# A gated state-space layer on one core: the second convolution tile moved to the gate's PSUM bank, and taps, z split and output product moved in the chunk step

## The reference

```
proj = xn @ in_proj.T                       # gate (4096), x (4096), B, C (8 x 128 each), dt (64)
x, B, C = silu(causal_conv4(proj))          # 4 taps per channel
state_t = state_(t-1) * exp(dt_t A) + dt_t x_t B_t
y_t = state_t C_t + D x_t                   # 64 heads of 64, in 8 groups
z = y * rsqrt(mean(y^2 in its group) + eps) * norm_weight * silu(gate)
out = z @ out_proj.T ;  x = x + out
```

## Time and profile before

| | |
|---|---|
| median of 3 runs | 1332.53 us (1332.19 to 1333.8) |
| profiled execution, its own time | 1333.64 us |
| its span, first to last instruction | 1331.9 us |
| mean granted TensorE clock | 0.979 of full speed |
| TensorE / VectorE / ScalarE / GpSimd busy | 1239.0 / 926.7 / 691.6 / 658.7 us |
| groups 1 to 6, each | 117.9 us |
| groups 0 and 7 with the handover | 61.9 to 176.3 us, 883.9 to 1008.0 us |

### The profile page before, as it was taken

One profiled execution on the slowest core, in us unless ns is written; L12 is line 12 of the kernel. 1 busy time (PEld: TensorE's weight loads), 2 busy tenths in 40 slices (PEclk: granted clock), 3 DMA queues, 4 the chain that ended last, 5 costly groups with the idle time before them and its releaser, 6 DMA issues.

```text
span 1331.9 us, 22035 instructions
## 1 busy us (share of the span) xinstructions
PE 1239.0 (93%) x6680; PEld 966.3 (73%) x6690; DVE 926.7 (70%) x1734; ACT 691.6 (52%) x1042; POOL 658.7 (49%) x707
## 2 busy tenths in 40 slices
PE   5999999999999999999999999998878999889976
PEld 4777777776777777777777777776666777667764
DVE  5786677667667766766776676677766655569995
ACT  3675666566656656675666567555523333222220
POOL 5056546654744665475465456543663434343330
PEclk9999999999999999999999999999989999999996
DMA  5111011011101201110010110010003233131100
GB/s 174 45 49 34 1 51 48 18 33 48 32 1 32 64 16 32 48 30 3 32 64 16 32 48 25 9 37 1 22 27 107 83 95 98 44 94 35 56 16 24
DMA packets 44233, 57.52 MB, mean 43 GB/s; under 512 B 10117, under 2 KB 21159, under 8 KB 43929
## 3 DMA queue, kind: packets, MB, share of 16 engines
q1 hardware_dynamic: 44185, 56.92, 14.0%
HBM read 49.95 MB, written 6.96 MB: 43 GB/s over the span
## 4 chain that ended last, share of the span: by engine, by line
PE 68%; DVE 11%; issue 9%; ACT 7%; POOL 2%; DMA 1%; DVEq 1%; SPq 1%; ACTq 0%; POOLq 0%
PE p_d L94 14%; PE p_d L98 7%; PE p_gate L94 6%; PE p_tile L94 5%; PE p_in L1092 4%; PE p_x L1100 4%; DVE conv L702 3%; PE p_y L1121 3%; PE p_gate L98 3%; PE p_tile L98 2%; PE t_p_a L1872 2%; PE p_y L94 2%; ACT L612 2%; PE t_p_c L1940 2%; PE p_in L94 2%
## 5 line engine op out<-in xcount | busy, mean ns | idle before, releaser
L702 DVE SCALAR_TENSOR_TENSOR conv<-p_tile,conv_taps,conv 128x511 f32<-128x511 f32 x189 | 141.4, 748 | 46.2 <-ACT conv L573 31.2
L812 DVE TENSOR_TENSOR em<-em,p_gb 128x512 f32<-128x512 f32 x128 | 82.1, 682 | 65.7 <-ACT em L612 65.7
L702 DVE SCALAR_TENSOR_TENSOR conv<-p_d,conv_taps,conv 128x511 f32<-128x511 f32 (+2 forms) x99 | 73.9, 747 | 65.8 <-ACT conv L573 61.9
L94 PE MATMUL p_d<-wr_hi,zt_hi 128*128 128x512 f32 x248 | 101.1, 408 | 13.1 <-DVE wr_lo L740 7.9
L94 PE MATMUL p_tile<-xn_hi,wc_hi 128*128 128x512 f32 x252 | 110.1, 437 | 0.8 <-DVE halo L706 0.8
L578 ACT ACTIVATE xbc<-conv 128x512 f32<-128x512 f32 x96 | 60.6, 631 | 94.2 <-DVE conv L710 57.9
L516 POOL TENSOR_TENSOR squares<-squares 128x256 f32<-128x256 f32 x64 | 47.7, 746 | 122.2 <-ACT squares L635 122.2
L485 POOL TENSOR_TENSOR x_w<-xs,head_g 128x512 f32<-128x512 f32 x56 | 59.2, 1057 | 98.3 <-ACT xs L606 97.8
L94 PE MATMUL p_gate<-xn_hi,wr_hi 128*128 128x512 f32 x248 | 104.2, 420 | 0.0
L635 ACT ACTIVATE squares<-y 128x512 f32<-128x512 f32 x64 | 40.5, 633 | 119.8 <-DVE y L845 116.4
L94 PE MATMUL p_tile<-xn_lo,wc_hi 128*128 128x512 f32 x252 | 98.5, 391 | 0.0
(11 more groups left out here) (361 smaller groups left out, 3511.8 us busy)
## 6 DMA issues: line engine op xcount, KB each, us to landing
w_raw<-w SPq DMA_DIRECT2D x108, 256.0 KB, 2.7
q_words<-q SPq DMA_DIRECT2D x33, 256.0 KB, 2.6
h_ring<-h_lo_rows SPq DMA_DIRECT2D x6, 704.0 KB, 4.8
h_lo_rows<-h_rest SPq DMA_DIRECT2D x11, 256.0 KB, 2.0
x_res<-x SPq DMA_DIRECT2D x8, 256.0 KB, 4.8
out<-out_t SPq DMA_DIRECT2D x8, 256.0 KB, 2.0
h_lo_rows<-h_rest SPq DMA_DIRECT2D x11, 128.0 KB, 1.8
gate_second<-w SPq DMA_DIRECT2D x4, 256.0 KB, 5.2
```

The source lines that it names most:

```text
L94: pe.matmul(out, lhs(k)[0], rhs(k)[n], start=(start and k == 0 and n == 0), stop=False)
L702: ve.scalar_tensor_tensor(out=conv[:, s, sh:], in0=p[:, 0:HALF - sh], scalar=conv_w[:, bass.ds(g, 1), j, tap], in1=conv[:, s, sh:], op0=AL ...
L812: ve.tensor_tensor(m, m, gm.unsqueeze(1).broadcast_to([P, HG // 2, P]), ALU.mult)\
```

## The change

Five edits, in all engines' programs at once:

1. The second convolution tile of a step (j = 1, 3) goes to p_gate; the gate product of a two-tile step goes to p_tile. Their waits follow: the second tile waits for the gate's silu or the previous tile's taps, the gate product for the first tile's taps.
2. VectorE takes the last taps of the second tile at the start of the next step (in step 0 all but the first tap), and ScalarE's silu of it comes there too, behind the exponentials. The decay product no longer waits for them.
3. z is rounded and split in its own step, right after the z product, not in the next one.
4. In two-tile steps the output product stands behind the second tile; elsewhere it stands ahead of the state product, now in the last half group too. The residual comes after the z product (in the last half group before y is summed); the row sum comes later (or, in the last half group, earlier and in another bank).
5. Of the four output weight tiles ScalarE rounds 12, 13, 10, 11 in one go in step 0; GpSimd scales and splits 12 and 13 (`out_rest`), VectorE splits 10 and 11. `norm` and the addition of x_d change places on GpSimd.

```diff
-    def out_bank(last, c):
-
-        return p_y if last and c == NC - 1 else p_d0
+    def ss_bank(last, c):
+
+        return p_gate[:, 0:1] if last and CH <= c < NC else p_gb[:, 3 * P:3 * P + 1]
+
+    def gate_bank(c):
+
+        return p_tile if c % CH < 2 else p_gate
 
     def bank_of(j):
...
-        return (p_tile, p_d1)[j in (1, 3)]
+        return (p_tile, p_gate)[j in (1, 3)]
...
-    VE_LO = list(range(TILES + KT, WT))
-    POOL_LO = list(range(TILES + KT))
-    FIRST = [0, 1, 2, 3, 6, 7, 8, 9, 4, 5]
+    OUT = TILES + KT
+    VE_LO = [OUT, OUT + 1]
+    POOL_LO = list(range(OUT)) + ["scaled", OUT + 2, "scaled", OUT + 3]
+    FIRST = [0, 1, 2, 3, 6, 7, 8, 9, 4, 5] + POOL_LO[OUT:]
+    ROUNDED = [OUT + 2, OUT + 3, OUT, OUT + 1]
...
-        return g * WT + (FIRST.index(w) if is_zero(g) and w in FIRST else w) + 1
+        if w >= OUT:
+            return g * WT + OUT + ROUNDED.index(w) + 1
+        return g * WT + (FIRST.index(w) if is_zero(g) else w) + 1
...
+                if c == 0:
+                    for w in (OUT + 2, OUT + 3):
+                        out_rest(g, w)
+                if last and c >= CH:
                     norm(n - 1, (c - 1) % 2)
                 if c > 0:
 
                     pool.wait_ge(s_t, st)
                     pool.wait_ge(s_xd, n + 1)
                     pool.tensor_tensor(y[:], y[:], x_d[:], ALU.add).then_inc(s_txd, 1)
-                if tail:
+                if not (isinstance(g, int) and n == 0) and not (last and c >= CH):
...
+        def out_rest(g, w):
+
+            raw = w_raw[:, w % RAW, :]
+            scale = norm_w[:, bass.ds(g, 1), w - OUT].broadcast_to([P, D])
+            pool.wait_ge(s_whi, hi_count(g, w))
+            pool.tensor_tensor(raw, raw, scale, ALU.mult).then_inc(s_wlo, 1)
+            done, count = lo_count(g, w)
+            pool.wait_ge(done, count - 1)
+            pool.tensor_tensor(lo_of(w), raw, hi_of(w).bitcast(F32), ALU.subtract).then_inc(s_wlo, 1)
...
-        up.rest(pool, 0, 0, 0)
         rstd_of(NC - 2)
         sum_squares(LAST)
+        up.rest(pool, 0, 0, 0)
         norm(LAST, (NC - 1) % 2)
...
-                for tile in left:
-                    tile_silu(*tile)
                 act.wait_ge(s_xt, n + 1)
                 wait(act, s_xdt, n)
                 act.activation(xs[:], p_x[:], ACT.Copy).then_inc(s_xs, 1)
-                if not first:
-                    z_round(n - 1, p_y)
...
+                for tile in left + now:
                     tile_silu(*tile)
                 for T, tg, j, _ in later:
                     tile_in(T, tg, j)
                 if c == 0:
                     wait(act, s_out, n)
-                    w_round(g, TILES + KT)
-                    w_round(g, TILES + KT + 1)
+                    for w in ROUNDED:
+                        w_round(g, w)
                 act.wait_ge(s_y, n + 1)
                 wait(act, s_ss, n)
                 act.activation(squares[:], y[:], ACT.Square).then_inc(s_sq, 1)
+                z_round(n, y_bank(last, c))
                 made = gate_tile(g, last, c)
                 if made:
-                    wait(act, s_z, n)
-                    gate_silu(CH + n, made[1], made[2])
-                if c == 0:
-                    w_round(g, TILES + KT + 2)
-                    w_round(g, TILES + KT + 3)
+                    gate_silu(CH + n, made[1], made[2], gate_bank(c))
...
-        z_round(LAST, y_bank(True, NC - 1))
+        up.round_w(act, 0, 0, 0)
...
-                _, now, later = conv_tiles(g, last, c)
+                left, now, later = conv_tiles(g, last, c)
                 tail = last and c >= CH
 
                 ve.wait_ge(s_gb, n + 1)
                 wait(ve, s_m, 2 * n)
                 ve.tensor_tensor(gm, p_gb[:, 0:P], tri[:], ALU.mult).then_inc(s_gm, 1)
                 ve.tensor_copy(b_tok[:], p_gb[:, P:2 * P]).then_inc(s_gm, 1)
-                if not first:
-                    z_rest(n - 1, p_y)
+                for tile in left:
+                    tile_taps(*tile, range(1 if c == 1 else 2, TAPPED[tile[3]]))
+                if tail:
+                    variance(n - 1, (c - 1) % 2, ss_bank(last, c))
                 for k in rows_in(last, c):
...
-                if not first and not tail:
-                    variance(n - 1, (c - 1) % 2)
+                if tail:
+                    residual(n - 1, c - 1)
+                    row_stats(c - 1)
...
-                if tail:
-                    variance(n - 1, (c - 1) % 2)
-                elif not first:
-                    residual(n - 1, (c - 1) % NC, p_d0)
                 for tile in later:
                     tile_taps(*tile, range(1))
-                if last and c == NC - 1:
-                    up.scale(ve, 0, 0, 0)
+                if not first and not tail:
+                    variance(n - 1, (c - 1) % 2, ss_bank(last, c))
...
-                if tail:
-                    residual(n - 1, c - 1, out_bank(last, c))
+                if not first and not tail:
+                    residual(n - 1, (c - 1) % NC)
                 for k in rows_in(last, c):
                     row_rest(k)
+                if last and c == NC - 1:
+                    up.scale(ve, 0, 0, 0)
+                z_rest(n, p)
...
-                if last and c > 0:
+                if last and 0 < c < CH:
                     row_stats(c - 1)
...
-                for tile in later:
-                    tile_taps(*tile, range(1, TAPPED[tile[3]]))
                 if c == 0:
-                    for k in range(GW // P):
-                        w_rest(g, TILES + KT + k)
+                    for w in VE_LO:
+                        w_rest(g, w)
+                else:
+                    for tile in later:
+                        tile_taps(*tile, range(1, 2))
...
-        z_rest(LAST, y_bank(True, NC - 1))
-        variance(LAST, (NC - 1) % 2)
+        variance(LAST, (NC - 1) % 2, ss_bank(True, NC))
...
+        def conv_tile(T, g, j, hf, bank=None, made=0):
+
+
+            if bank is not None:
+                wait(pe, s_tap, TAPS * (j - 1))
+            elif j in (1, 2, 4):
+                wait(pe, s_sg, made)
             else:
-                wait(pe, s_tap, TAPS * (j - 1))
+                wait(pe, s_tap, tapped(g, hf, {3: 2}.get(j, j)))
...
+                tg, j, hf = tile
+                if c % CH < 2:
+                    pe.wait_ge(s_tap, tapped(tg, hf, 2 * j) + TAPPED[hf])
+                elif c % CH == 2:
+                    pe.wait_ge(s_tap, tapped(tg, hf, 4))
+                else:
+                    pe.wait_ge(s_sg, CH + n)
+                gate_product(*tile, gate_bank(c))
+
+        def sum_rows(m, ss):
...
-                for _, tg, j, hf in left:
-                    pe.wait_ge(s_tap, tapped(tg, hf, j) + TAPPED[hf])
...
-                    conv_tile(*tile)
-                if c == 1:
-                    pe.wait_ge(s_whi, (g + 1) * WT)
-                    pe.wait_ge(*lo_count(g, WT - 1))
-                if not first and not tail:
+                    conv_tile(*tile, made=CH + n)
+                if tail:
+                    pe.wait_ge(s_sg, LAST + 1)
+                    wait(pe, s_v, n - 1)
+                    sum_rows(n - 1, ss_bank(last, c))
+                if not first and not later:
                     pe.wait_ge(s_e, 2 * n + 1)
                     out_product(n - 1, p_d0)
-                    pe.wait_ge(s_m, 2 * (n + 1))
-                    sum_rows(n - 1)
...
-                if last and c == NC - 1:
-                    pe.wait_ge(s_e, 2 * (n + 1))
-                    pe.wait_ge(s_res, n - 1)
-                    up.spread(pe, 0, 0, 0)
-                if later:
-                    pe.wait_ge(s_e, 2 * (n + 1))
                 for tile in later:
-                    conv_tile(*tile)
+                    conv_tile(*tile, made=CH + n)
+                if c == 1:
+                    pe.wait_ge(s_whi, (g + 1) * WT)
+                    for w in (VE_LO[-1], WT - 1):
+                        pe.wait_ge(*lo_count(g, w))
+                if not first and later:
+                    pe.wait_ge(s_e, 2 * n + 1)
+                    out_product(n - 1, p_d0)
 
                 pe.wait_ge(s_m, 2 * (n + 1))
-                if tail:
-                    sum_rows(n - 1)
+                if not first and not tail:
+                    sum_rows(n - 1, ss_bank(last, c))
...
-                if tail:
-                    if c < NC - 1:
-                        pe.wait_ge(s_e, 2 * (n + 1))
-                    out_product(n - 1, out_bank(last, c))
                 next_gate(g, last, n, c)
...
-        pe.wait_ge(s_sg, LAST + 1)
+        pe.wait_ge(s_res, LAST)
+        up.spread(pe, 0, 0, 0)
+        pe.wait_ge(s_v, LAST)
         pe.wait_ge(l2_lo, NC - 2)
         up.spread(pe, 0, 1, 1)
+        sum_rows(LAST, ss_bank(True, NC))
+        out_product(LAST, p_y)
         row_transpose(NC - 2, LAST)
-        sum_rows(LAST)
-        out_product(LAST, p_y)
```

36 lines of the change are left out of this document (11 added, 25 removed).

## The result

The changed kernel takes 1338.31 us (median of 15 runs, 1334.06 to 1339.94); the kernel before took 1332.66 beside it (15 runs, 1331.80 to 1334.34). The ratio is 1.0036, with a 95% interval from 1.0028 to 1.0044: slower by 0.36%. The prediction was 1318, in a range from 1303 to 1329, with 0.10 for slower. It was wrong in sign and outside its range.

A forecast was written before the change was run, and what follows sets the result against it. TensorE, busy 93% of the span, was taken as the bound, with only idle and low-clock time to win. Groups 1 to 6 -4.6, group 0 -1.2, group 7 -0.1, last half group -9: -14.9, giving 1318, range 1303 to 1329.

The forecast's parts named there:

- The second tile's bank: Second tile in p_gate: decay product no longer waits for its taps, nothing lost; steps 2, 5, 6 gain 2.77 per group.
- The chain from step 0 to step 1: Late output product, ScalarE rounding, four GpSimd instructions, norm, then residual: step 1's decay product starts at 312.7, unhindered 309.9.
- The length of step 1: Middle groups' step 1 becomes 20.0 instead of 18.08, 2.0 lost; bounds 18.5 and 21.0.
- the lower bound: Step 1 of the middle groups if the chain meets no contention: 18.5, 0.5 lost.
- Group 0: Step 1 taken unchanged; -0.8 for step 2 and -0.4 for steps 5 and 6, together -1.2.
- Step 4: No cost taken; longer than 15.7 would mean a late gate silu or residual, margin only 0.3 to 0.6 us.
- The last half group: Output product fills TensorE's gap before the transposes: step 4 to 10.0, steps 4 to 6 to 33.0; -9 taken with handover.
- may fall as often as before: In the last half group the clock may fall as often as before, giving -5.0 instead of -12.0.
- -5 to -12 for the tail: Last half group with handover: -12.0 at full clock, -5.0 by the clock column; -9 taken.
- The weak tail: Rival: VectorE's queue and low clock limit the last half group to -4, 1323 in all, or 1329 without group gains; chance 0.2.
- the dear scaled product: Rival: GpSimd's one-value-per-partition product costs more than 1.06; at 3.0 us, step 1 grows 3.9, time 1345; chance 0.1.
- the listed signs: If right: residual wait 2 to 3, tap wait 1 to 2 in step 1, GpSimd full, steps 2 and 6 full.
- the signs that it is wrong: Step 1 under 18 or over 21 us; steps 0 and 4 longer than 14.6 and 15.7.

The follow-up runs named there:

- The first experiment: Changed kernel with GpSimd making the norm in step 0 ahead of its four output weight instructions; 1313.7 us, ratio 0.9855.
- the four built on it: On the norm-first kernel: decayed state early, 1316.2 us; that with old last half group, 1317.5; decayed state plus later VectorE rest, 1308.8; that plus two tail moves, 1304.1.
- the last one: Changed kernel with only two last-half-group moves: squares ahead of rstd on GpSimd, row splits ahead of y and z on VectorE; 1330.5 us, ratio 0.9978.
- The two moves of the last experiments: Last half group: GpSimd squares ahead of rstd and decayed state, VectorE row splits ahead of y and z; 1304.1 us with earlier edits, 1330.5 alone on changed kernel.
- the fastest one: Changed kernel with norm and decayed state early on GpSimd, one VectorE rest behind step 1's left taps, and two last-half-group moves; 1304.1 us, ratio 0.978.
- the kernel with the decayed state early: Norm-first kernel with GpSimd also making step 1's decayed state in step 0, ahead of norm and output weight rests; 1316.2 us, ratio 0.9881.

## Why the prediction was wrong

The forecast sum was -14.9 us, and the span grew by 5.6. Two terms of the sum carry most of the 20.5 us between them: the last half group with its handover (11.3) and groups 1 to 6 (6.9).

*The second tile's bank.* Right. The wait for taps before the decay product is gone and nothing took its place in steps 2, 3, 5 and 6. The six steps other than 1 and 4 give 3.2 per group where 2.77 was forecast.

*The chain from step 0 to step 1.* Its mechanism was right in each link, and its first length too: the decay product was forecast 2.8 late and waits 2.71. GpSimd's four instructions take 4.95 plus gaps where 5.0 with 0.45 for contention was put. The first experiment, which takes the norm out of this chain, shows it: the wait goes everywhere.

*The length of step 1.* This is the term that was mis-sized: 21.1 on average, not 20.0, so 3.0 lost per group, not 2.0 (20.0 - 18.08 is 1.92; the sum took 2.0). That is 6.1 us more than forecast in groups 1 to 6, where 6.9 was missed in all; step 4, below, adds 3.4, and the other six steps take off 2.5. Two sizes failed. The short taps were put at 1.05; they took 3.38 in three of the groups (2, 3 and 6), where GpSimd's weight rests of step 1 lie beside them, and the second tile waited 2.36, not 1.5. And the sum kept TensorE at full clock, since the earlier trace rows shows 1.00 in every step: in seven of the eight groups it fell once in step 1, at 1.5 us each. Groups 1, 4 and 5 took the forecast 20.0 by luck, for another reason than forecast: no wait for taps (18.5, the lower bound), plus one fall of the clock. In the middle groups the fall needs the 2.71 wait: in the kernel with the norm first, the four built on it, and the one with four splits on VectorE, which all remove it, the clock falls in no step 1 of groups 1 to 6. But the wait does not make the fall certain, since group 6 of the changed kernel has both long waits and no fall, and it is not the only thing that brings one: group 0 has no such wait, only waits of 0.21, 0.45 and 1.32, and its clock fell in three of the profiled kernels (the changed one, the one with the norm first and the last one) and not in four others with the same waits. What else decides it is open.

*Group 0.* "I take it unchanged" was wrong for step 1: 19.97 against 18.13. It has the fall too; in the four profiles with the same waits and no fall it is 18.5.

*Step 4.* Its cost was taken at nothing, with a margin of 0.3 to 0.6. With the output product behind the second tile, the state product comes 2.8 us earlier, and waits 0.45 for ScalarE's exponentials. Step 4 is 0.56 longer, 3.4 us in the six groups. Undone alone, most of the gain is lost again in step 5.

*The last half group.* The step that failed most. The prediction's working for step 4, "output product to 6.15", followed ScalarE's exponentials and left out the row sum that stands ahead of the product in the diff, with GpSimd's queue behind it. It gave 10.0 for step 4; 16.28 came. The two moves of the last experiments gave 3.95 back. They were only run together; of the two, the squares ahead of the row's rstd and the decayed state on GpSimd is the one that bears on this wait, and with it step 4's row sum does not wait. The waits for the row splits in steps 5 to 7 were forecast and are there (2.46, 1.99, 1.74). With the waits came low clock: 0.79 and 0.76 in steps 4 and 5, where the earlier trace rows shows 0.87 over the three steps. So the reading that the clock "may fall as often as before" was right in kind and too mild, and -5 to -12 for the tail was wrong in sign: steps 4 to 7 with the handover took 2.3 more.

*The rivals.* The weak tail was nearest for the tail, with the wrong sign; the dear scaled product did not come true (1.04 for it, against 1.06 taken). Slower was given 0.1, and came by mechanisms that none of the rivals had.

*What would show each step.* Of the listed signs, the residual wait, GpSimd's full queue and full steps 2 and 6 were seen; the wait for left taps came in three of the six groups, and was 2.36 instead of 1 to 2. Of the signs that it is wrong, a step 1 over 21 us holds in three of six groups, and a step 4 over 15.7 in all six (16.3), though not for the reason given there: the state product waited for ScalarE's exponentials, not for a gate's silu or the residual.

*Left open.* The feed-forward part, whose code is the same, took 323.9, 325.3 and 328.8 in the kernels before, after and in the fastest one, at mean clocks of 0.95, 0.95 and 0.94. In the other kernels it took 325.3 to 328.8, in no order that follows the edits: 328.8 with the norm first, 325.9 when the decayed state was moved as well. Why it differs was not tried; up to 3.5 us between two profiles can lie there and not in the edit.

## What to carry to other kernels

Before work is moved to an engine, list what stands behind it in that engine's queue, and who waits for that: here 5 us on an engine half idle held up a norm of 0.55 us and so the fullest engine, and putting the norm first turned a loss of 0.4% into a gain of 1.4%. Where a product is put into a gap, follow every instruction that stands ahead of it on its engine down to its own producer, the small row sum too. And price an idle stretch on TensorE above its length: in five of the six middle groups a step with a wait of 2.7 us also had a fall of the clock, which cost another 1.5.

## What was not expected of the hardware

Three VectorE taps of 3, 2 and 1 columns, whose inputs conv and halo both lie in SBUF, took 0.74 together in step 0 of the kernel with the decayed state early, where GpSimd stood still:

```profile
414.00 0.74 DVE L724 SCALAR_TENSOR_TENSOR conv<-halo,conv_taps,conv 128x3 f32<-128x3 f32 x3
```

That is 0.22 each. In the changed kernel's step 1 they took 0.94, 1.18 and 1.18, the first beside GpSimd's x_d product of 1.03, the others beside its two subtractions of 1.26: nearly the length of one GpSimd instruction each, and not in proportion to their size. The Trainium skill, page "SBUF — State Buffer", section "Who interferes with whom", has a VectorE instruction with two SBUF inputs and a GpSimd instruction that reads SBUF exclude each other. The trace agrees, and adds that a tap of 0.22 pays up to 0.96 more, where the z product of 0.70 paid 0.73 more in the earlier trace rows.

A fall of the clock could also save time: in the groups where it fell early, GpSimd's weight work came after the short taps and not beside them, and step 1 was shorter (20.0) than in the one without a fall (21.2).
